# The threshold search of a router: five-way in 14 rounds in place of four-way in 16

## What is computed

```
logits = x_flat @ Wr                       # 12552 x 8
probs = softmax(logits, axis=0)            # over the tokens
vals, idx = top_k(probs.T, 1024)           # each expert takes its 1024 best tokens
selected = x_flat[idx]
h = gelu(einsum(selected, W1) + b1)
out_e = einsum(h, W2) + b2
output = zeros.at[idx].add(vals * out_e)
```

## Time and profile before

| | us |
|---|---|
| median of 3 runs | 2658.64 (2657.56 to 2659.1) |
| the profiled execution | 2655.75 |
| its span | 2653.6 |
| VectorE busy in the span | 2253.0 (85%) |
| TensorE busy in the span | 2267.6 (85%) |
| first count of the search to the end of the last accumulator read | 1489.75 to 1544.83 |

### The profile page before, as it was taken

One profiled execution on the slowest core, in us unless ns is written; L12 is line 12 of the kernel. 1 busy time (PEld: TensorE's weight loads), 2 busy tenths in 40 slices (PEclk: granted clock), 3 DMA queues, 4 the chain that ended last, 5 costly groups with the idle time before them and its releaser, 6 DMA issues. The chain is left out here.

```text
span 2653.6 us, 26586 instructions
## 1 busy us (share of the span) xinstructions
PE 2267.6 (85%) x6899; PEld 1106.0 (42%) x6899; DVE 2253.0 (85%) x3620; ACT 1604.3 (60%) x3048; POOL 2067.7 (78%) x1107
## 2 busy tenths in 40 slices
PE   5999999999999999999997307852799999999997
PEld 2444444444444444444443103321455555555554
DVE  2999999999999999999999682223799998999985
ACT  4776777777777677677675214433555555655543
POOL 2889889889988988998988107876788887888872
PEclk8999999999999999999999658975899999999999
DMA  2233333333333334334333202431111111111110
GB/s 78 90 119 115 97 117 111 104 106 115 104 106 122 97 104 126 102 97 123 110 95 99 90 0 57 66 44 28 28 33 33 38 36 35 36 32 32 33 31 18
DMA packets 180610, 199.44 MB, mean 75 GB/s; under 512 B 40062, under 2 KB 170988, under 8 KB 180332
## 3 DMA queue, kind: packets, MB, share of 16 engines
q1 hardware_dynamic: 169196, 189.35, 23.4%
q0 software_dynamic: 11264, 8.40, 2.4%
HBM read 164.44 MB, written 33.25 MB: 75 GB/s over the span
## 5 line engine op out<-in xcount | busy, mean ns | idle before, releaser
L915 POOL TENSOR_TENSOR a_hc<-a_h,a_cs 128x896 f32<-128x896 f32 (+1 forms) x448 | 860.3, 1941 | 55.9 <-DVE a_h L778 55.5
L362 PE MATMUL a_y_bank<-a_hc,a_ident 128*128 128x448 f32 (+1 forms) x1792 | 740.3, 543 | 21.9 <-DVE a_yz L798 21.3
L553 ACT ACTIVATE a_da<-a_dt,a_neg_a 128x448 f32<-128x448 f32 (+1 forms) x896 | 551.9, 631 | 296.3 <-DVE a_h L778 291.2
L778 DVE TENSOR_TENSOR_SCAN a_h<-a_da,a_h,a_dbx 128x448 f32<-128x448 f32 x528 | 584.9, 1141 | 9.5 <-ACT a_da L553 4.4
L362 PEld LDWEIGHTS a_y_bank<-a_hc,a_ident 128*128 128x128 f32 x1792 | 330.9, 190 | 325.8 <-issue 272.3
L1781 PE MATMUL c_p_E<-c_w_ex,c_hid 128*128 128x512 f32 x800 | 374.8, 602 | 15.8 <-DVE c_sc L2036 12.3
L2186 POOL TENSOR_TENSOR c_prod<-c_prob,c_qkv 128x1024 f32<-128x1024 f32 x100 | 280.8, 2834 | 114.6 <-DVE c_prob L2060 114.6
L762 DVE TENSOR_TENSOR a_dbx<-a_dtx,a_b_bank 128x896 f32<-128x896 f32 (+1 forms) x308 | 329.8, 1071 | 16.2 <-PE a_b_bank L355 16.0
L903 POOL TENSOR_TENSOR a_dbp<-a_dtx,a_bs 128x896 f32<-128x896 f32 (+1 forms) x140 | 271.5, 1939 | 0.0
L778 DVE TENSOR_TENSOR_SCAN a_h<-a_da,a_h,a_dbp 128x448 f32<-128x448 f32 x240 | 264.6, 1139 | 0.0
L2177 POOL TENSOR_TENSOR c_prod<-c_qkv 128x1024 f32<-128x1024 f32 x100 | 232.3, 2357 | 21.4 <-ACT c_qkv L1849 21.2
(11 more groups left out here) (309 smaller groups left out, 3643.0 us busy)
## 6 DMA issues: line engine op xcount, KB each, us to landing
a_cs<-c_rows SPq DMA_DIRECT2D x96, 896.0 KB, 5.3
a_bs<-c_rows SPq DMA_DIRECT2D x24, 1120.0 KB, 5.6
a_cs<-c_rows SPq DMA_DIRECT2D x16, 900.0 KB, 4.4
c_x<-h_rows SPq DMA_DIRECT2D x100, 64.0 KB, 2.3
heads<-c_ot SPq DMA_DIRECT2D x25, 256.0 KB, 2.0
c_dealt<-heads SPq DMA_DIRECT2D x200, 32.0 KB, 1.9
rolled<-c_res SPq DMA_DIRECT2D x25, 256.0 KB, 2.4
h_rows<-a_th SPq DMA_DIRECT2D x24, 224.0 KB
```

The costliest lines, as they stand in the source:

```text
L362: pe.matmul(y_bank[:, d, 0:g.w], ident[:], hc[:, (g.i * NS + n) % HC_RING, d, 0:g.w], start=(n == 0), stop=(n == NS - 1)).then_inc(s_sum, 1)
L553: act.activation(da[:, k % DA_RING, 0:g.w], dt[g.slot][:, d, 0:g.w], ACT.Exp, scale=neg_a[:, d * NS + n:d * NS + n + 1]).then_inc(s_da, 1)
L778: dve.tensor_tensor_scan(h[:, n, d, 0:g.w], da[:, (g.i * 2 * NS + k) % DA_RING, 0:g.w], x, state, ALU.mult, ALU.add).then_inc(s_scan, 1)
L915: pool.tensor_tensor(hc[:, (q.i * NS + n) % HC_RING, :, 0:q.w], h[:, n, :, 0:q.w], cs[:, n % C_RING, 0:q.w].unsqueeze(1).to_broadcast([P, ...
```

## The change

Each round tries four levels in place of three and cuts the range in five. VectorE counts under levels 1 and 2 as before, ScalarE under levels 3 and 4, one Sign behind the other into seen_a and the new tile seen_b, each with its own column of reach. Seven rounds of base 5 cover 78125 values, so each half takes 7 rounds and ROUNDS is 14. The matmul has four columns and writes p_small from column 128; TensorE waits for two ScalarE increments a round. The limits of columns 3 and 4 are both those of sums of signs; the limit of the low half is made for two columns by one instruction as before. The table steps has 7 x 5 columns in place of 8 x 4. The buffer of the first level of the low half follows the parity of the round. The extra work inside rounds stays tied to rounds 0 to 6, DIGITS and DIGITS + 1, so the memset of round 6 is now in the last round of the high half.

```
--- before.py
+++ after.py
@@ -999,7 +999,7 @@
     WIDE = CAP + SPAN
     HALF = CAP // 2
     HT = TILES // 2
-    DIGITS = 8
+    DIGITS, RADIX = 7, 5
     LANE = 16 * SPAN
     XG = 3
 
@@ -1013,6 +1013,7 @@
     seen = [sb(f"seen{k}", [P, SPAN]) for k in range(2)]
     seen_a = sb("seen_a", [P, SPAN])
     tmp_a = sb("tmp_a", [P, SPAN])
+    seen_b = sb("seen_b", [P, SPAN])
     ones = sb("ones", [P, SPAN])
     gt = sb("gt", [P, SPAN])
     eq = sb("eq", [P, SPAN])
@@ -1032,12 +1033,12 @@
     ident = sb("ident", [P, P])
     small = sb("small", [P, 16])
     bits = sb("bits", [P, 6], I32)
-    steps = sb("steps", [P, DIGITS, 4])
-    level = [sb(f"level{k}", [P, 4]) for k in range(2)]
-    around = sb("around", [P, 4])
-    limit = [sb(f"limit{k}", [P, 3]) for k in range(2)]
-    reach = sb("reach", [P, 3])
-    over = sb("over", [P, 3])
+    steps = sb("steps", [P, DIGITS, RADIX])
+    level = [sb(f"level{k}", [P, RADIX]) for k in range(2)]
+    around = sb("around", [P, RADIX])
+    limit = [sb(f"limit{k}", [P, RADIX - 1]) for k in range(2)]
+    reach = sb("reach", [P, RADIX - 1])
+    over = sb("over", [P, RADIX - 1])
     passed = sb("passed", [P, 1])
     above = sb("above", [P, 1])
     found = sb("found", [P, 4])
@@ -1114,10 +1115,10 @@
             dve.wait_ge(s_dve, count[0])
 
         for r in range(DIGITS):
-            for k in range(4):
-                dve.memset(steps[:, r, k:k + 1], float(k * 4 ** (DIGITS - 1 - r)))
+            for k in range(RADIX):
+                dve.memset(steps[:, r, k:k + 1], float(k * RADIX ** (DIGITS - 1 - r)))
         dve.memset(limit[0][:, 0:2], float(LANE - CAP))
-        do(dve.memset(limit[0][:, 2:3], float(LANE - 2 * CAP)))
+        do(dve.memset(limit[0][:, 2:4], float(LANE - 2 * CAP)))
         do(dve.tensor_scalar(level[0][:], steps[:, 0, :], -32768.5, None, ALU.add))
         dve.wait_ge(s_x, 16)
         do(dve.tensor_scalar(x[:], x[:], 0.0, None, ALU.add))
@@ -1141,11 +1142,11 @@
 
         def decide(r, lim):
             dve.wait_ge(s_pe, pe_round(r))
-            do(dve.tensor_tensor(over[:], p_small[:, 129:132], lim[:], ALU.is_le))
+            do(dve.tensor_tensor(over[:], p_small[:, 128:132], lim[:], ALU.is_le))
             do(dve.tensor_reduce(passed[:], over[:], AX.X, ALU.add))
-            size = float(4 ** (DIGITS - 1 - r % DIGITS))
+            size = float(RADIX ** (DIGITS - 1 - r % DIGITS))
             if r % DIGITS + 1 < DIGITS:
-                do(dve.scalar_tensor_tensor(out=level[(r + 1) % 2][:], in0=passed[:].to_broadcast([P, 4]), scalar=size,
+                do(dve.scalar_tensor_tensor(out=level[(r + 1) % 2][:], in0=passed[:].to_broadcast([P, RADIX]), scalar=size,
                                             in1=around[:], op0=ALU.mult, op1=ALU.add))
                 progs["n_level", r + 1] = count[0]
             else:
@@ -1181,7 +1182,7 @@
         do(dve.tensor_scalar(found[:, 2:3], found[:, 0:1], 0.5, None, ALU.add))
         do(dve.scalar_tensor_tensor(out=own[:], in0=high[:], scalar=found[:, 2:3], in1=low[:], op0=ALU.is_equal,
                                     op1=ALU.mult))
-        do(dve.tensor_scalar(level[0][:], steps[:, 0, :], 0.5, None, ALU.add))
+        do(dve.tensor_scalar(level[DIGITS % 2][:], steps[:, 0, :], 0.5, None, ALU.add))
         progs["n_level", DIGITS] = count[0]
         do(dve.tensor_scalar(seen[0][:], high[:], found[:, 2:3], 0.0, ALU.is_gt, ALU.add, accum_out=above[:]))
         progs["n_above"] = count[0]
@@ -1191,8 +1192,8 @@
             if r == DIGITS:
                 dve.wait_ge(s_pe, PE_ABOVE)
                 do(dve.tensor_scalar(limit[1][:, 0:2], limit[0][:, 0:2], p_max[:, 132:133], None, ALU.add))
-                do(dve.scalar_tensor_tensor(out=limit[1][:, 2:3], in0=p_max[:, 132:133], scalar=2.0,
-                                            in1=limit[0][:, 2:3], op0=ALU.mult, op1=ALU.add))
+                do(dve.scalar_tensor_tensor(out=limit[1][:, 2:4], in0=p_max[:, 132:133].to_broadcast([P, 2]),
+                                            scalar=2.0, in1=limit[0][:, 2:4], op0=ALU.mult, op1=ALU.add))
             if r == DIGITS + 1:
                 do(dve.tensor_copy(bits[:, 0:1], found[:, 2:3]))
                 do(dve.tensor_scalar(bits[:, 1:2], bits[:, 0:1], 16, None, ALU.logical_shift_left))
@@ -1287,8 +1288,9 @@
         act.wait_ge(s_dve, progs["n_high"])
         for r in range(ROUNDS):
             act.wait_ge(s_dve, progs["n_level", r])
-            act.activation(seen_a[:], (high if r < DIGITS else own)[:], ACT.Sign, scale=-1.0,
-                           bias=level[r % 2][:, 3:4], accum_out=reach[:, 2:3]).then_inc(s_count, 1)
+            for k, seen_k in ((2, seen_a), (3, seen_b)):
+                act.activation(seen_k[:], (high if r < DIGITS else own)[:], ACT.Sign, scale=-1.0,
+                               bias=level[r % 2][:, k + 1:k + 2], accum_out=reach[:, k:k + 1]).then_inc(s_count, 1)
         act.wait_ge(s_dve, progs["n_negmax"])
         act.activation(tmp_a[:], x[:], ACT.Exp, bias=small[:, 1:2], accum_out=small[:, 2:3]).then_inc(s_act, 1)
         act.preload_act_table_set("gelu_and_others")
@@ -1314,8 +1316,8 @@
 
         def count_mm(r):
             pe.wait_ge(s_dve, progs["n_reach", r])
-            pe.wait_ge(s_count, r + 1)
-            pe.matmul(p_small[:, 129:132], group[:], reach[:], start=True, stop=True).then_inc(s_pe, 1)
+            pe.wait_ge(s_count, 2 * r + 2)
+            pe.matmul(p_small[:, 128:132], group[:], reach[:], start=True, stop=True).then_inc(s_pe, 1)
 
         for r in range(DIGITS):
             count_mm(r)
```

## The result

| | before | changed |
|---|---|---|
| median of 12 runs, us | 2658.30 (2655.75 to 2660.95) | 2652.14 (2648.24 to 2656.05) |
| ratio | | 0.9973, 95% interval 0.9966 to 0.9981 |
| the profiled execution, us | 2655.75 | 2652.93 |
| its span, us | 2653.6 | 2650.8 |

Forecast 2652.8 in 2650.8 to 2656.0, measured 2652.14; the medians lie 6.2 us apart, for a forecast of 5.8. The 0.2% that the prediction names as the bound of no change lies just inside the interval, at its smaller end.

What follows compares the result with a forecast made beforehand. The prediction took the search, paced by VectorE's two counts a round, to bound the span: 6.58 us from two rounds less, minus 0.78 for TensorE's wait, saves 5.8, so median 2658.64 becomes 2652.8 us, range 2650.8 to 2656.0.

Steps and rivals of the forecast that it cites:

- Two rounds less: Threshold search: one round fewer in each half, 3.26 us in the high and 3.32 in the low, 6.58 saved.
- The tie: Each search round: ScalarE's second Sign starts at 0.95 and ends at 2.00 us, against VectorE's 1.99.
- The rival of reads in series: ScalarE's two counts cannot overlap: 0.26 us a round, 3.1 lost, 3.5 saved, 2655.2 us; chance 13%.
- The wait: TensorE's counting matmul passes two semaphore waits: starts 0.065 us later in 12 rounds, 0.78 us lost.
- The transpose of the earlier trace: First-stage turn_norm, ScalarE releasing TensorE's second wait last: start 0.11 to 0.12 us behind, taken as the nearer row.
- The wider forms: Matmul, comparison, sum, next level and around gain one column: costed at nothing, bounds 0 to 0.01 us a round.
- The fills: Set-up: three more one-column memsets hidden in the wait for x's DMA, cost 0, at most 0.09 us.
- The sum: Whole kernel: 6.58 us gained less 0.78 lost gives 5.8 us saved, median 2652.8, 0.22% less.
- The signs: Timeline checks: low-half round about 3.39 us, TensorE's start 2.05 to 2.12, first indirect DMA about 1592.2, later gap unchanged to 1.
- The givers-back: Last stage, shifted against TensorE's clock, loses two or three microseconds, some 2655.5 us; chance 14%.
- the slower rival: Last stage: TensorE reaches full clock later; 16 us more at the lower level loses 8, giving 2660.8; chance 6%.

Runs made afterwards that it cites:

- base 7: Changed kernel with six levels a round, three each on VectorE and ScalarE, 12 rounds: 2656.54 us, ratio 0.9992 to the kernel before.
- the first two groups: Follow-up kernels run beside the kernel before, on two chips; the kernel before took 2659.67 and 2659.03 us there.
- three on VectorE: Changed kernel with levels 1 to 3 counted by VectorE and only level 4 by ScalarE: 2665.48 us, ratio 1.0029 to the kernel before.

## Why the prediction was right

- Two rounds less: forecast 6.58, and the rounds that are left are the same but for the terms below. The last round of the high half took the memset without cost, 0.58 us idle left.
- The tie: forecast that ScalarE would end at 2.00 and VectorE at 1.99. Measured 1.97 to 1.98 for ScalarE and 1.99 for VectorE. The second Sign's read comes 0.84 behind its start and not 0.86, and takes 0.19. The rival of reads in series is refuted by the 0.95 (0.94 in base 7) from start to start.
- The wait: forecast 0.065 a round in 12 rounds, 0.78. Measured 0.04 to 0.05 in the profile; half a microsecond in all, both by undoing it (51.26 to 50.81) and by adding it alone (57.30 to 57.79). That the wait written second costs more stands by the swapped order; that it is passed as a step of its own is my reading, which no row shows. Two things made the term smaller than forecast. ScalarE ends 0.02 earlier. And the count of 12 rounds was too large by three: in rounds 3 to 5 of the kernel before the comparison did not wait for TensorE but for VectorE's own work on the keys (its row ends at 1503.19 and the comparison starts at 1503.22), so those rounds grew by 0.01 to 0.02 and the other nine by 0.05. The transpose of the earlier trace rows was the right row to read it from: 0.11 to 0.12 there, 0.11 here.
- The wider forms: costed at nothing with 0.01 a round as the bound; from the comparison to the next Sign it is 0.59 in place of 0.58, in the level's instruction, at or a little under the bound.
- The fills: forecast hidden behind the transfer of x. They are, just: in one profile VectorE idles 0.17 us for the transfer, in the other it starts 0.03 behind the level, and from the issue of x it is then 3.68, where it was 3.69 before.
- The sum: forecast 5.8 for the search, 6.04 in the profiles, 6.2 between the medians. The search is the part that was understood. That the medians came within half a microsecond of it was in part luck: their interval is 5.1 to 9.0 us, and the same kernel run again lay 8.4 under the kernel before. The forecast on the median and not on the profiled execution was right for a reason that I did not have: the profiled execution of before had an indirect stage 3 to 5 us shorter than the profiles of the first two groups, which would put it at the low edge of its kernel's runs.
- The signs: the second Sign at 0.95, TensorE at 2.09 and a round of 3.38 came as said, and the first indirect DMA at 1592.58 for 1592.2. Two did not. TensorE's start is laid to VectorE and not to ScalarE. And the gap from the first indirect DMA to the end, which was to stay the same to 1 us, grew by 2.6 (1055.6 to 1058.2): 4.5 more with the stall, 1.9 less in the last stage. The prediction had no term for a stage that varies by itself.
- The givers-back: the last stage was shorter by 1.9, not longer, and with 13 us more ahead of it (three on VectorE) it took 846.2. Among the profiles it lies between 842.6 and 852.5 with no relation to when it starts. No run showed what the slower rival describes.
- What I did not see: that the step whose time the search most depends on after the counts, the three instructions of the decision, had 0.19 us a round to give, four times what the wait cost.

## What to carry to other kernels

When an engine idles inside a latency loop, price a second piece of work on it by the rows of two such instructions in a row: if both engines then end together, the work is nearly free, and the same work on the other engine costs its full length a round (here 0.95 against 0.04). Where two engines' results are joined, let them raise one semaphore; here a second wait that came late or level cost 0.04 to 0.06 us each time. And when two single profiles disagree with the medians, cut both at the same marks first: the stage that was edited repeated to hundredths here (in one case to 0.2 us), and the rest tells how much one profile can prove.

## What was not expected of the hardware

In two kernels here an instruction with an accumulator output on four columns cost no more than one without, though the next one waits for the accumulator: the read of 0.08 us starts 0.09 into the pass of 0.16, and the next instruction 0.20 after the start of the pass. Of two waits ahead of a TensorE instruction, the one written second, when it decides, is followed by the start after 0.11 to 0.12 us, and the first after 0.05 to 0.06. And TensorE's rows ended up to 8 us before ScalarE, which waits for the result, was released, in all eight profiles of two groups of runs and in none of the four of a third; the cause is open.
